# Three bias-row additions to residuals issued on GpSimd in place of VectorE, in a four-layer graph network on one core

## The reference, cut to what matters

```python
h = relu(layernorm(einsum('mn,bnf->bmf', L_norm, x) @ Wc + bc, g1, be1))
x1 = h + x
... attention over 4 heads gives o ...
x2 = layernorm(x1 + o @ Wo + bo, g2, be2)
m = gelu(x2 @ W1 + b1) @ W2 + b2
layer1 = layernorm(x2 + m, g3, be3)
x = layernorm(x + layer1)
```

## Time and profile before

| | us |
|---|---|
| median of 3 runs | 2137.61 |
| lowest, highest | 2133.22, 2139.08 |
| the profiled execution, own time | 2134.39 |
| its span in the profile | 2132.6 |
| busy: PE, DVE, ACT, POOL | 1985.8, 1773.5, 1454.2, 189.8 |

### The profile page before, as it was taken

The page is one execution under the profiler, slowest core; times in us unless marked ns, Lnnn a source line. Parts: engine busy times, 40 slices in busy tenths (PEclk is TensorE's granted clock), DMA queues, the critical chain, the costliest instruction groups (busy, mean ns, idle before and its releaser), DMA issues.

```text
span 2132.6 us, 86379 instructions
## 1 busy us (share of the span) xinstructions
PE 1985.8 (93%) x37353; PEld 1749.7 (82%) x37353; DVE 1773.5 (83%) x5049; ACT 1454.2 (68%) x4411; POOL 189.8 (9%) x252
## 2 busy tenths in 40 slices
PE   6979679999999999999999999999999999999986
PEld 3444358989898989889998989898989898899975
DVE  6779677888888988898888988888889888988855
ACT  5657336767777676767677777677776777676764
POOL 2000000010101010101010110101010001010100
PEclk9999779999999999999999999999999999999998
DMA  7857300000100001000100010001000010000000
GB/s 281 291 179 271 106 1 22 5 20 3 42 3 22 3 3 42 13 12 3 42 13 12 3 41 8 18 3 42 3 22 3 3 42 13 12 3 13 3 12 12
DMA packets 36824, 87.82 MB, mean 41 GB/s; under 512 B 2416, under 2 KB 26992, under 8 KB 32752
## 3 DMA queue, kind: packets, MB, share of 16 engines
q1 hardware_dynamic: 36464, 82.56, 11.2%
HBM read 52.15 MB, written 30.41 MB: 39 GB/s over the span
## 4 chain that ended last, share of the span: by engine, by line
PE 46%; DVE 27%; ACT 10%; issue 3%; POOL 1%; POOLq 0%; DVEq 0%; ACTq 0%
PE ps L247 14%; PE ps L249 13%; PE ps L248 13%; DVE stats L1562 4%; ACT pool_mem L1438 3%; DVE pool_mem L1716 2%; DVE hl_a L1614 2%; PE ps L1180 2%; DVE pool_mem L1703 1%; DVE t L1583 1%; DVE pool_mem L1697 1%; DVE mv L1566 1%; PE ps L261 1%; DVE pool_mem L1701 1%; DVE t L1593 1%
## 5 line engine op out<-in xcount | busy, mean ns | idle before, releaser
L1438 ACT ACTIVATE pool_mem<-ps,lstm_b 128x64 f32<-128x64 f32 (+2 forms) x2496 | 607.7, 353 | 120.0 <-PE ps L249 113.2
L247 PE MATMUL ps<-hl_a,w_hi 128*128 128x64 f16 (+2 forms) x3776 | 541.9, 214 | 32.2 <-DVE hl_a L611 16.0
L248 PE MATMUL ps<-hl_a,w_hi 128*128 128x64 f16 (+2 forms) x3776 | 540.4, 214 | 0.0
L249 PE MATMUL ps<-hl_a,w_lo 128*128 128x64 f16 (+2 forms) x3776 | 540.2, 214 | 0.0
L247 PEld LDWEIGHTS ps<-hl_a,w_hi 128*128 128x128 f16 x3776 | 349.1, 97 | 66.7 <-DVE hl_a L611 17.1
L247 PE MATMUL ps<-hl_b,w_hi 128*128 128x84 f16 (+2 forms) x2112 | 368.0, 229 | 5.0 <-DVE hl_b L1727 3.4
L248 PE MATMUL ps<-hl_b,w_hi 128*128 128x84 f16 (+2 forms) x2112 | 368.6, 229 | 0.0
L249 PEld LDWEIGHTS ps<-hl_a,w_lo 128*128 128x128 f16 x3776 | 349.0, 97 | 23.7 <-issue 1.7
L249 PE MATMUL ps<-hl_b,w_lo 128*128 128x84 f16 (+2 forms) x2112 | 367.4, 229 | 0.0
L248 PEld LDWEIGHTS ps<-hl_a,w_hi 128*128 128x128 f16 x3776 | 349.1, 97 | 20.7 <-issue 1.1
L247 PE MATMUL ps<-pool_mem,w_hi 128*128 128x64 f16 (+2 forms) x3072 | 352.0, 200 | 2.4 <-DVE pool_mem L1721 1.3
(11 more groups left out here) (232 smaller groups left out, 4328.0 us busy)
## 6 DMA issues: line engine op xcount, KB each, us to landing
xa<-in_x SPq DMA_DIRECT2D x32, 512.0 KB, 5.6
h_scratch<-pool_mem SPq DMA_DIRECT2D x14, 1024.0 KB, 4.3
pool_mem<-h_scratch SPq DMA_DIRECT2D x14, 1024.0 KB, 7.3
pool_mem<-in_wpack SPq DMA_DIRECT2D x16, 704.0 KB, 4.2
out<-xb SPq DMA_DIRECT2D x16, 512.0 KB, 3.2
o_scratch<-act_in SPq DMA_DIRECT2D x14, 512.0 KB, 3.1
act_in<-o_scratch SPq DMA_DIRECT2D x14, 512.0 KB, 5.4
row<-in_rows SPq DMA_DIRECT2D x1, 1408.0 KB, 11.4
```

The source lines that it names most:

```text
L247: nc.tensor.matmul(o, l[0], r[0], start=first, stop=False, skip_group_check=True)
L248: nc.tensor.matmul(o, l[0], r[1], start=False, stop=False, skip_group_check=True)
L249: return nc.tensor.matmul(o, l[1], r[0], start=False, stop=last, skip_group_check=True)
L1438: op = nc.scalar.activation(gates[s][h][:, g, m * w:(m + 1) * w], gate_place(s, h, g, m, w), ACT.Tanh, bias=lstm_b[:, bias:bias + 1], scal ...
```

## The change

The three additions leave VectorE's program and enter GpSimd's, at the same names in `ROUND`: `add_bias` runs there at `turn_x1` and `turn_x2`, `shift_xa` at `xa_bias`. The operation (a `tensor_tensor` add of 128x512) and the semaphore that it raises stay. `add_bias` now waits for the transposes of TensorE itself (`feat_ps`); before, it stood behind `low`, which waited for ScalarE. `shift_xa` waits for the same two signals as before.

```diff
+                def add_bias(s, n, h, which):
+
+                    pool.wait_ge(*feat_ps.at(s, n, h, which))
+                    nc.gpsimd.tensor_tensor(x1[s][:, blocks(h), :], x1[s][:, blocks(h), :], half_row(RESIDUAL_BIAS[which]),
+                                            ALU.add).then_inc(biased.of(s, h), 1)
+
+                def shift_xa(s, n, h):
+                    pool.wait_ge(*feat_ps.at(s, n, h, "xp"))
+                    pool.wait_ge(*x_ok.at(s, n, h, "x1"))
+                    nc.gpsimd.tensor_tensor(xa[s][:, blocks(h), :], xa[s][:, blocks(h), :], half_row("be3"), ALU.add)\
+                        .then_inc(pre_ok.of(s, h), 1)
+
                 def run(name, s, n):
                     base, h = step_of(name)
                     if base in NORM_OF:
                         ln_root(s, n, h, NORM_OF[base])
+                    elif base == "turn_x1":
+                        add_bias(s, n, h, "x1")
+                    elif base == "turn_x2":
+                        add_bias(s, n, h, "x2")
+                    elif base == "xa_bias":
+                        shift_xa(s, n, h)
...
                     nc.vector.tensor_tensor(lo, src, hi, ALU.subtract).then_inc(feat_lo.of(s, h), 1)
-                    if which in RESIDUAL_BIAS:
-                        add_bias(s, n, h, which)
```

More of the change, by code:

```diff
@@ L1614, in low @@
                     nc.vector.tensor_tensor(lo, src, hi, ALU.subtract).then_inc(feat_lo.of(s, h), 1)
-                    if which in RESIDUAL_BIAS:
-                        add_bias(s, n, h, which)
-                def add_bias(s, n, h, which):
-                    nc.vector.tensor_tensor(x1[s][:, blocks(h), :], x1[s][:, blocks(h), :], half_row(RESIDUAL_BIAS[which]),
-                                            ALU.add).then_inc(biased.of(s, h), 1)
                 def conv_bias(s, n, h):
@@ L1676, in add_mlp @@
                                                                      x1[s][:, blocks(h), :], ALU.mult, ALU.add))
[L1678 to L1682, removed]
                 def add_xa(s, n, h):
@@ L1770, in run @@
                         add_y(s, n, h)
-                    elif base == "xa_bias":
-                        shift_xa(s, n, h)
                     elif base == "norm_l0":
```

## The result

The changed kernel takes 2175.86 us (median of four, 2174.36 to 2179.23), the kernel before 2136.45 (median of four, 2133.22 to 2139.08). The ratio is 1.0186, 95% interval 1.0170 to 1.0202: 39 us slower. The sign was forecast; the size was not, and the time lies 3 us above the range. The profiled execution after has a span of 2177.4 us.

A forecast was written before the change was run, and what follows sets the result against it. It took TensorE and VectorE as both nearly full, the chain changing between them. A and B, 2.1 us a round x 7 = +14.7 us on 2137.6, gave 2152 us, with a range of 2127 to 2173.

The forecast's parts named there:

- What leaves VectorE: 96 additions leave VectorE's queue: 65.6 us busy, 58 us of queue, of which 8.4 us come off the chain.
- The exclusion: GpSimd instructions reading SBUF and VectorE instructions with two SBUF inputs block each other fully; each addition costs up to 1.1 us.
- The mark of 65 us: Sign in the profile after: the forecast is wrong if VectorE's busy time falls by the whole 65 us.
- The length of an addition: One 128x512 addition on GpSimd taken as 1.1 us, with 1.0 and 1.5 us as bounds.
- A: The two additions on the chain, blocking VectorE's splits L1727 and cell products: each costs 1.1, gives 0.6; +1.0 us in sum.
- B: `turn_x2` of stream 0, half 1: the addition blocks L1719 and L1721 ahead of low part L1614; +1.1 us on the chain.
- C: Stream 1's `xa_bias` and `turn_x1`: two additions block splits L1727, L1614 ends 1.6 us later, 0.85 covered, 0.75 not.
- D: Stream 0's `xa_bias` and `turn_x1`: L1614 ends 1.6 us after 1159.79; 1.2 us covered, 0.4 not.
- Elsewhere the block is small or nothing: Remaining places, judged where VectorE takes one-input statistics behind transposes: the full 0.60 us is won, but TensorE doesn't wait there.
- the rival in which all passes with a slow addition: At 1.5 us per addition, all four places' delays pass: 6.05 x 7 = +42 us, 2180 us; slow end's chance 0.08.
- Swallowed: Rival: delays vanish in TensorE's waits for ScalarE, as in layer 3's attention; 2134 to 2143, about 2138 us; chance 0.21.
- no exclusion: Rival: both engines read side by side, or GpSimd gives way between elements; -8.4 us, 2129 us; chance 0.23.

The follow-up runs named there:

- the useless addition: Kernel before, VectorE keeping its additions, plus a 128x512 addition on GpSimd that nobody reads, at the same 96 places with the same waits: 2207.67 us, 1.0332.

## Why the prediction was right in its sign and too small

- **What leaves VectorE** was right: 58 us of queue, and 8.4 us on the chain; left out altogether, the additions give 8 us.
- **The exclusion** was right, in both directions and in what it hits. VectorE's busy time grew, as one of the signs had it ("falls by much less than 65 us or grows"). The mark of 65 us was too high: without the additions and without any block it falls by 49.6 us.
- **The length of an addition** was mis-sized: 1.1 us, taken as nearer to the one row with two inputs; the estimate of 1.12 us beside it was as short. It is 1.26 us at the least, and 1.36 in the median with its own waits. The bound of 1.5 held it. This adds 0.16 to each block: at 1.26 A is +1.3, not +1.0.
- **A** held at about its size: +0.81 + 0.71 - 0.25 = 1.3 us (the -0.25 is there with the additions left out too, so it is won by the freed VectorE). **B** came as forecast, 1.07 us for 1.1.
- **C and D were left out of the value**, and this is the second step that failed. C made 0.61 (0.75 worked out), and in the way that was said: the three splits took 3.00 us together for 0.98. D made 0.99 (0.4). Together that is 1.6 us in each round, 11 us. They were set to nothing as "the difference of two like numbers", though at 1.0 us per addition they still came to 0.55 and 0.2; the range had them, at 8 us. D went another way than was said. The low part was not the first that TensorE missed: the chain after has L1706 with 1.42 us and L1708 with 1.38, then ScalarE's tanh L1447, and behind it in ScalarE's queue the copy of the keys, L1402, for which the scores wait:

```profile
1179.67 1.42 DVE pool_mem L1706
1181.12 1.38 DVE pool_mem L1708
1182.52 0.42 ACT pool_mem L1447
1182.94 0.50 ACT pool_mem L1402
...
1183.57 1.15 PE ps L1180 x32
```

- **A place that was priced at nothing: the step that put the time outside the range.** "Elsewhere the block is small or nothing" covered stream 1's `xa_bias` and `turn_x1` of half 0, near 1036 us, and these are the largest jump, 0.35 + 1.36 us, a third of the round's loss and 12 us over seven rounds. The one other place that had been looked at was the earlier trace rows, where VectorE takes statistics, and it was taken for all. With `be3` alone on GpSimd the same place shows 0.36 + 0.41 us. Without this place the jumps come to 3.9 us in a round, 28 us, 2165 us: inside the range. The prediction's own sum says the same: with 1.26 us per addition, and C and D in full, it is 1.32 + 1.26 + 1.07 + 0.72 = 4.4 us in a round, 31 us, 2168 us. I had looked for low parts that TensorE waits for; here it is the other stream's LSTM cell that is held (L1708, L1724), and TensorE waits for that. VectorE's queue is shared by four strands, and a block delays whatever is in it.
- **The sum** of the eight jumps, 5.65 us, is near the 6.05 of the rival in which all passes with a slow addition; that rival's 2180 us was nearer than the forecast. That was luck in the number: it reached this from A to D at 1.5 us; the chip had 1.26 us and one place more. The range ended below it, at 2173, since I gave it 0.08.
- **Swallowed** and **no exclusion** are both refuted: the second by the useless addition, 73 us slower; the first by the fact that hardly any jump is taken back.

## What to carry to other kernels

Work moved to GpSimd isn't off VectorE's hands while it reads SBUF: each instruction of it can hold VectorE's next two-input instruction, or cast, for its whole length, here 1.3 us to save 0.6. Where such a move is wanted, start each piece when VectorE is about to read PSUM or take statistics, and check the length of VectorE's untouched instructions in the profile, not its total. Shorter pieces shorten each block, but here they took back only a third of the loss. When pricing delays on a queue that several strands share, follow every strand that the delayed instruction holds up, other engines' queues too, and count a block that exceeds its margin as passed on.

## What the runs showed of the hardware

- The exclusion is for whole instructions and in both directions: a 128x512 addition on GpSimd takes 1.26 us alone and up to 1.53 beside VectorE; a VectorE product of 0.42 us takes up to 1.51. Cut in half, the most is 0.97. The Trainium skill (SBUF — State Buffer, "Who interferes with whom") states this rule, and these numbers agree with it.
- A fill on GpSimd (0.52 us, nothing read) left two-input products at 328 and 326 ns, but raised the casts from 245 to 289 ns in the mean. Two fills in a row held a cast of 0.25 us for both, up to 1.01 us.
- A tiny operation of VectorE with one SBUF input and an SBUF output, 128x2, is held by an addition on GpSimd as well (213 ns for 170 in the mean), which I had not expected of an instruction of that size.
